# Row sums of two softmaxes on VectorE in place of ScalarE's accumulator, in a two-layer decoder

## What is computed

```python
def _layernorm(x, axis=-1, eps=1e-05):
    m = jnp.mean(x, axis=axis, keepdims=True)
    v = jnp.var(x, axis=axis, keepdims=True)
    return (x - m) / jnp.sqrt(v + eps)
...
    def _L0_xattn_ref(query, key, value, cell_mask, seq_mask, W_k, b_k, W_o, b_o):
        ...
        k_proj = jnp.einsum('bkd,qd->bkq', key, W_k) + b_k
        scores = jnp.einsum('bqd,bkd->bqk', query, k_proj)
        scores = scores + jnp.log(cell_mask) + jnp.log(seq_mask)[:, None, :]
        p_attn = jax.nn.softmax(scores, axis=-1)
        x = jnp.einsum('bqk,bkd->bqd', p_attn, value)
        return jnp.einsum('bqd,od->bqo', x, W_o) + b_o
...
    def _L1_xattn_ref(query, key, value, Wq, bq, Wk, bk, Wv, bv, Wo, bo):
        ...
        Q = jnp.einsum('bsd,de->bse', query, Wq) + bq
        K = jnp.einsum('bsd,de->bse', key, Wk) + bk
        V = jnp.einsum('bsd,de->bse', value, Wv) + bv
        scale = 1.0 / jnp.sqrt(jnp.asarray(D, Q.dtype))
        scores = jnp.einsum('bqd,bkd->bqk', Q, K) * scale
        attn = jax.nn.softmax(scores, axis=-1)
        out = jnp.einsum('bqk,bkd->bqd', attn, V)
        return jnp.einsum('bsd,de->bse', out, Wo) + bo
...
    x = _layernorm(x + _L0_attn_ref(x, L0_attn_w_qkv, L0_attn_w_conv1), axis=-1)
    x = _layernorm(x + _L0_xattn_ref(x, ctx_1024, ctx_1024, mask_BxSxS2_ff1, mask_BxS2_ff1, L0_xattn_W_k, L0_xattn_b_k, L0_xattn_W_o, L0_xattn_b_o), axis=-1)
    x = _layernorm(x + _L0_ffn_ref(x, L0_ffn_Wg, L0_ffn_Wq, L0_ffn_Wk, L0_ffn_Wv, L0_ffn_Wo), axis=-1)
    x = _layernorm(x + _L1_attn_ref(x, L1_attn_Wq, L1_attn_bq, L1_attn_Wk, L1_attn_bk, L1_attn_Wv, L1_attn_bv, L1_attn_Wo, L1_attn_bo), axis=-1)
    x = _layernorm(x + _L1_xattn_ref(x, ctx_1024, ctx_1024, L1_xattn_Wq, L1_xattn_bq, L1_xattn_Wk, L1_xattn_bk, L1_xattn_Wv, L1_xattn_bv, L1_xattn_Wo, L1_xattn_bo), axis=-1)
    x = _layernorm(x + _L1_ffn_ref(x, L1_ffn_w_int8, L1_ffn_weight_scale, L1_ffn_bias), axis=-1)
```

## Time and profile before

| | us |
|---|---|
| median of 3 runs | 848.61 |
| lowest and highest | 847.72, 851.18 |
| the profiled execution's own time | 853.0 |
| its span in the trace | 851.1 |

### The profile page before, as it was taken

How to read it: one execution, slowest core, us unless ns; L and a number is a source line. 1 busy time by engine, 2 the same in 40 slices (tenths; PEclk the granted TensorE clock), 3 DMA queues, 4 the chain that set the end, 5 groups by cost and what they waited for, 6 DMA issues and landing times.

```text
span 851.1 us, 20772 instructions
## 1 busy us (share of the span) xinstructions
PE 785.4 (92%) x8013; PEld 606.1 (71%) x8013; DVE 654.7 (77%) x1973; ACT 488.7 (57%) x1509; POOL 359.3 (42%) x604
## 2 busy tenths in 40 slices
PE   8989999998887999999989899999999899999992
PEld 4566787765766778766767688776777688777771
DVE  6163888787787698788778779789769879888676
ACT  3126445686556445577655554588655645587654
POOL 0088312306676523403775632402777633202465
PEclk7799999999999999999999999999999999999996
DMA  9893000001353000000236000001244200000001
GB/s 222 240 288 154 2 2 2 1 3 56 113 191 135 23 2 2 1 3 29 97 134 220 29 12 2 1 2 29 60 170 154 78 2 2 2 2 2 2 1 39
DMA packets 23074, 53.31 MB, mean 63 GB/s; under 512 B 3888, under 2 KB 9680, under 8 KB 22976
## 3 DMA queue, kind: packets, MB, share of 16 engines
q1 hardware_dynamic: 22976, 51.99, 19.1%
HBM read 48.67 MB, written 3.31 MB: 61 GB/s over the span
## 4 chain that ended last, share of the span: by engine, by line
PE 64%; DVE 16%; POOL 8%; ACT 7%; issue 3%; DMA 1%; SPq 0%; DVEq 0%; ACTq 0%; POOLq 0%
PE psum L429 11%; PE psum L434 11%; PE psum L473 8%; PE psum L630 5%; PE psum L652 5%; PE psum L459 4%; PE psum L643 4%; DVE bn L930 2%; ACT x L710 2%; POOL rstd L1199 2%; PE psum L466 2%; PE psum L565 2%; POOL xplus L1206 1%; PE psum L424 1%; PE psum L574 1%
## 5 line engine op out<-in xcount | busy, mean ns | idle before, releaser
L710 ACT ACTIVATE x<-res,ez,rstd 100x256 f32<-100x256 f32 x160 | 86.7, 593 | 65.4 <-POOL ez L1202 65.2
L473 PE MATMUL psum<-eT,ctx 128*128 128x100 f32 x768 | 95.2, 280 | 1.3 <-DVE eT L956 1.3
L473 PEld LDWEIGHTS psum<-eT,ctx 128*128 128x128 f32 x768 | 92.4, 197 | 2.5 <-DVE eT L956 1.7
L1197 POOL TENSOR_SCALAR ve<-mv 100x2 f32<-100x2 f32 x96 | 22.4, 233 | 163.2 <-DVE mv L933 159.1
L704 ACT ACTIVATE eT<-psum 100x400 f32<-100x400 f32 (+3 forms) x128 | 61.7, 495 | 43.7 <-PE psum L466 19.5
L459 PE MATMUL psum<-ctxT,qT 128*100 128x361 f32 x256 | 84.9, 474 | 1.5 <-ACT qT L704 1.1
L816 ACT ACTIVATE work<-psum,mx 100x100 f32<-100x100 f32 x256 | 67.5, 365 | 21.7 <-DVE mx L1112 21.5
L1185 POOL TENSOR_TENSOR kT<-cell,kT 100x722 f32<-100x722 f32 x12 | 20.7, 1722 | 131.5 <-ACT cell L684 131.5
L704 ACT ACTIVATE xT<-psum 128x400 f32<-128x400 f32 (+2 forms) x80 | 35.5, 445 | 69.0 <-PE psum L589 25.7
L1199 POOL TENSOR_TENSOR rstd<-ve,minus_half 100x2 f32<-100x2 f32 x96 | 70.1, 730 | 8.0
L930 DVE BATCH_NORM_STATS2 bn<-res 100x6 f32<-100x256 f32 x192 | 71.2, 412 | 0.0
(11 more groups left out here) (243 smaller groups left out, 2028.1 us busy)
## 6 DMA issues: line engine op xcount, KB each, us to landing
ctx<-in_ctx SPq DMA_DIRECT2D x16, 768.0 KB, 7.0
ctxT<-in_ctxT SPq DMA_DIRECT2D x16, 722.0 KB, 5.0
cell<-in_cell SPq DMA_DIRECT2D x12, 282.0 KB
seq<-in_seq SPq DMA_DIRECT2D x12, 282.0 KB
x<-in_x SPq DMA_DIRECT2D x16, 200.0 KB
out<-vs SPq DMA_DIRECT2D x16, 200.0 KB
eT<-agent_rows SPq DMA_DIRECT2D x12, 200.0 KB
work<-in_x SPq DMA_DIRECT2D x4, 384.0 KB
```

What stands on the lines that cost most here:

```text
L473: last = e.matmul(bk[b][:, c * S:(c + 1) * S], s.ctx[:, b, j, c * P:(c + 1) * P], s.pT[:, b, j, :], start=j == 0, stop=j == S2C - 1)
L710: e.activation(dst[0:S, b, :], s.res[0:S, b, :], ACT.Identity, scale=s.rstd[:, b:b + 1], bias=s.shift[:, b:b + 1]).then_inc(*act.up(f"x{b}"))
```

## The change

Three edits and a table. ScalarE's exponential loses `accum_out`. VectorE gets a `tensor_reduce` with add, over 100 x 2 x 361 elements of `s.p`, that writes both batches' sums at once; it stands behind the wait for the second exponential, raises a new step "su", and the reciprocal waits for this step. The step lists of the stages first and second on VectorE get the name "su". The sequences of all five engines are new.

```diff
--- before.py
+++ after.py
@@ -85,10 +85,10 @@
     "start": "bias weights",
     "mask": "zero clip",
     "mix": NORM,
-    "first": "mx0 nb0 mx1 nb1 pT0 rs aT1 " + NORM,
+    "first": "mx0 nb0 mx1 nb1 pT0 su rs aT1 " + NORM,
     "pick": "z0 z1 gp gt tie0 tie1 rk0 rk1 pk0 pk1 kT vs1 mx0 su0 mx1 su1 sm0 sm1 rd eT1 aT " + NORM,
     "local": "k0 k1 k2 k3 v1 " + " ".join(f"ma{i} mb{i} eT{i} rd{i} aT{i}" for i in range(NB * NC)) + " " + NORM,
-    "second": "mx0 nb0 mx1 nb1 pT0 rs aT1 " + NORM,
+    "second": "mx0 nb0 mx1 nb1 pT0 su rs aT1 " + NORM,
     "quant": "am am2 am3 sc y0 y1 up0 up1 yq0 yq1 os " + NORM,
 }
 GPSIMD = {
@@ -738,8 +738,7 @@
                 for b in range(NB):
                     e.wait_ge(*dve(f"nb{b}", t))
                     src = s.p[:, b, 0:S2] if stage == "first" else bk[b][0:S, 0:S2]
-                    e.activation(s.p[:, b, 0:S2], src, ACT.Exp, bias=s.nbias[:, b:b + 1],
-                                 accum_out=s.sum[:, b:b + 1]).then_inc(*act.up(f"ex{b}"))
+                    e.activation(s.p[:, b, 0:S2], src, ACT.Exp, bias=s.nbias[:, b:b + 1]).then_inc(*act.up(f"ex{b}"))
                     yield
                 e.wait_ge(*pe("pT1", t))
                 copy(s.pT[:, 1, :, :].rearrange("p j t -> p (j t)"), bk[1][:, 0:S2C * S]).then_inc(*act.up("pT1"))
@@ -956,6 +955,8 @@
                 e.tensor_copy(s.pT[:, 0, :, :].rearrange("p j t -> p (j t)"), bk[0][:, 0:S2C * S]).then_inc(*dve.up("pT0"))
                 yield
                 e.wait_ge(*act("ex1", t))
+                e.tensor_reduce(s.sum[:, :], s.p[:, :, 0:S2], AX, ALU.add).then_inc(*dve.up("su"))
+                e.wait_ge(*dve("su", t))
                 e.reciprocal(s.rsum[:, :], s.sum[:, :]).then_inc(*dve.up("rs"))
                 e.wait_ge(*pe("av1", t))
                 e.tensor_copy(s.aT[:, :, S:2 * S], bk[1][:, 0:NC * S].rearrange("p (c t) -> p c t", c=NC)).then_inc(
@@ -1409,39 +1410,39 @@

...
-        "BACDABABCBCADADBCBAABDCAACABCDCBCBDADDACDDABABCAABBACADCBBACDABBCACDBDCBCABCDDADCBDAADACBDBDAACBACAC"
...
+        "BACDABBABCCADADCBDAABACBAACBDBCCCBDADDCDADABABCAABBACADCBBACBDACACBDBDCBACBCDDACADDBADACBDAADBCBACCD"
...
```

More of the change, by code:

```diff
@@ L1411 @@
     "PE": (
-        "BACDABABCBCADADBCBAABDCAACABCDCBCBDADDACDDABABCAABBACADCBBACDABBCACDBDCBCABCDDADCBDAADACBDBDAACBACAC"
-        "DCBDBCABDDBCACBACBDCBABCCBCDADCDACDBABCADBCDABACADCBCADBCABDDABDCDADBADAAAADABCBBDBCBBABABCCDCDCCDCC"
-        "BAABADDDADADBDBACCAABBABBCCDBDBCABACACACCDCCDAABDBBDCBABBADDDCDDACBCADBACDCDBDCBCABDDCACADBADCADBDBA"
-        "BCDACCBADCACBBDBDCADBCDCABCABDADBCDBAACDABCADBDCABDCABCADCABBCBDDAACBADCADCAABCBAABABCDDCDBBBDBCBDAA"
-        "DCCDCCBBCDACADDDAADDBAACACBAABBBBBBCDCDBACAACACCCCDCDBADBABDBACDDDDADCBBACACBDCCADBDCBDBACBDDCADCABD"
@@ new lines @@
+        "ACBDCBABDDBCACBCADBCBABDCCBCDACDACDABCBABDCDABACADCBCACDBABDABDDCDABADDAAADAABCBBDCBBBAABBCCDCDCCDCA"
+        "BCABDADDADDDABBACCAABBABBBDCCDBCABCAAACCCDCACDABDBBBDABBCDDCDDADACACBBDCACDDBDCBACBDDCACABDADCADBBDA"
+        "BCDACBACCDACBBDBACDDBCDCBACABDADBCDBAACDABCADBDCABDACBCADCACDBBBDAABCADACDCBAABCAABACBDDCDBBBDBCBDAA"
+        "DCDCCCBBDACACDDADDBADAACCBAAABBBBBCBCDDACBAACCACCCDCDABDBABBDACDDDCDADBBACACDBCCADBDCBDBCABDDCACABDD"
+        "ACDBBCDADBCCAABACBDACBDBDBACCADCADBBCBADDBDACADCACBABDDCBDAABCACDBACDBDCABDACBACCDBACBAAADAADBCBBDCD"
@@ new lines @@
+        "BABBBACDCDCCCCDABCBAAADDDDADADBCACAABBBBBBDCDCBACABCAACDCCCCDAABDBABDDBCADDDDBABCACBCBDACBDCDBDCACBD"
+        "DCABCADADCADBDAABCDABCABDCCBCBDACBCDADBCDABCDBADBDCABCADACBBADCDABDABACCDCABCBDDBDCABCADCACADABADBAA"
+        "ACDBCBDCBBBBACCDBDACCDCCDDDDBDDBCCDD"),
+    "DVE": (
+        "BACBDCDCADAAABBBCCDACAADBDACBCABADBCDBDCBACACAAADADBBDAACBABBCBABBCCBDDCCCCBDCDDADDDAADACBADBACCBABA"
+        "DCBCBCADBBCDACBACDBACBCDBCCDADABDCAABCDABBCACDACACDDBBBDBDDDAAACDACADABABBADBDBBCCACACBBCDCBDDCAABDA"
+        "DCDCAABDBCBDABDBAACABCCDACACBCBABCADDABBACDCBADBABDDACBDDCDABBCCCBCDCDCBDDCDAADDDACADBABDCBACBACCABD"
+        "BDBCCBADDABCCADBADBBACDDACAABDCCBDABBCAADCADCCBBBDBAADCACDDCCABABABDDDBDBAABACCBCADBCBDCDCBAADCDACDC"
+        "AAABDBBCDBABADACCBCDAACBCBCBDDCACAADBACDDABADBABDBDCCBDCABBCBCDCDCCBDCDADDDDCDABAADBCABABCCBACABDCBA"
+        "DBCADBDCBCADABDBADCADCABDACCBDABBAADDCACBDCCBDBBACACDADCCAAADBBDBAADBDBBCACCBACBCDBCDABDCAADCDDACAAD"
+        "CBBBDADABACDBCCABCACBCBABDDCACBDBACDADAADABBDBBDCCBBDABCCDCCDCCBDCDADDDADCAADBADBACBBACACBCDBCADBBCD"
+        "DACCBADABDBCABDADCABACDCBADBACDBDCACBDCBDCBDCDAAACADAABDBABDCACBBCBACBDDCCDBDCDDBDCDCD"),
@@ new lines @@
+    "ACT": (
+        "BAABCBADAACBADBCDBACBDDCACACBBCDCDADABDBACACBABADADCCBAABBCADBDBCADCBCADACDBACBDDAABDACCBCDDCBDABABC"
+        "CDACBBDBCCACDBDACBACBCDDADAABCCBABCADADAADBBDADAACDABCBBAABCBCBBACDDCCBDCABCDADABDACADBDACDABABACBDB"
+        "DBCBBCDBCACACCADACCDACBDBDCDCBDBADBADDBCAACBDCDADDBCBCACBDACDADBCDABBDACDBACACDBCDBBADCAADCCBBDDDBCA"
+        "CACABBBDDDAAACCCBBADDBACDAABACCAABABCADBBCBDCBDBACABDDCDABBCCDADCCADBAADBDADCCABAABCDADBBCBBBCBCAADC"
+        "CACCADCBCDDBADDCBDDCBAADBADCABDCBDACDCBDBCADBACCABDDDCBDBCADBCCAAADBCDBCDBACAADCBBBDDCDAAACCBBDDBADA"
+        "CACBCBADBDDAACCAACBABBADDABBCADCBACBABBCDCADDCBCBCACDADABAADBDACDCADAABCBDDBCBBBBACDCABCDCCAACDCDACB"
+        "BDDACBDBDCADBADACDBBDCBACBDDACBCDACCBADBDCDADABACDABCCDDBCBBACCADACDBBDDBCDACAACBBDDBADAACCCBBDBDDCA"
+        "CACADABAADBDAABCBCBAACBCBCDBCADDCBDACBDDDDCCBDDBCDCD"),
@@ L1439 @@
     "POOL": (
-        "BABCAADCDBABCCDDABCDABACBADCDBDACAAABBBABCCCABDAACDCDBADBBADACBCCBDBDCDCACDBDDCADABACBDCADDCBAAABABB"
-        "BCCCBCADAADCDBABDBDABACBCCDBDCDACCDBDDCADBACBDABCACDDAAABABBBCBCCACDAADCDBDABBADABCCCBBDCDDACCDDDBCA"
-        "DBACBADCDDBACAABCBBACAACDDBBDABCCCDBDDCD"),
+        "BABCAADCDBABCDCDABCDABAACBDACBDCDAAABBBABCCCABDAACCDDBABBDADACBCCBDBDCDCACDBDDCADABACBDBCACDAADABBAB"
+        "BCCCBCDAAADDBCADBBDABACBCCDBCDDACCDBDDCADBAACBADCCDAABABABBBCBDCCACDAADCDBDABBADABCCCBBDCDDACCDDDBCA"
@@ L1443 @@
+        "DBACBABDCDACABACBCBADAACDDBABDBCCCDBDDCD"),
     "SP": (
-        "ABCDAABCABACDBCDDBCDAABBCADACBCDDBCDABABCACBDDDCBACD"),
+        "ABCDABABAACCDCDBDBCDABABACBCDCADDBCDABACBACDDCBDABCD"),
 }
```

20 lines of the change are left out of this document (removed).

## The result

The changed kernel takes 862.86 us, median of 3 runs (859.42 to 863.64), against 848.61 before: a ratio of 1.0157, 95% interval 1.0111 to 1.0203. That is 14.3 us slower. The prediction was 850.5 us with a range to 858.5: wrong in size, and outside its range.

What follows compares the result with a forecast made beforehand. TensorE, busy 785.4 of 851.1 us, was taken as the bound, so only work in front of it counts. Reads -2.4 and remaining sums +4.3 make +1.9 us: 848.6 becomes 850.5 us, 8-in-10 range 843 to 858.5.

Steps and rivals of the forecast that it cites:

- The order at 0 +-3 us: New interleaving of the four streams in the engines' sequences: no block of TensorE's work saved, priced 0 +-3 us.
- The reads, -2.4 us: 64 accumulator reads leave ScalarE; TensorE released 0.10 us earlier in 24 waits for exponentials: 2.4 us gained, bounds 0 to 4.6.
- 12 us less busy time: Sign that the forecast is right: ScalarE's busy time down by 12 us.
- the 21.3 us that I had named: Sign that the forecast is right: TensorE's wait for the exponentials near 21 us, from 23.9 before.
- The sum, 0.90 us: Each of VectorE's 32 new sums over 722 columns takes 0.90 us, priced from the maximum; cheap alternative near 0.6.
- Hidden, 10.0 us: On VectorE the sums fill 10.0 us of the 17.5 us that the copy aT waited in 14 places.
- The rest, 20.4 x 0.21 = 4.3 us: The 20.4 us of sums left in VectorE's queue, priced by its chain share over busy share, 0.21: 4.3 us lost.
- The sums land on TensorE: Slower rival, chance 0.32: sums not in VectorE's waits delay other streams and reach TensorE; ten of 18 give +7.1, about 855.7 us.
- The exponential was the bottleneck: Faster rival, chance 0.20: earlier release and new order take 8.0 us off TensorE's wait for exponentials, sums cost 2: 842.6 us.

Runs made afterwards that it cites:

- nosum_oldorder: The kernel before without the accumulator and without any row sum (the reciprocal reads a tile of ones), old sequences: 852.58 us, ratio 1.0016.
- sum_oldorder: The changed kernel with all five sequences of the kernel before (sums on VectorE, no accumulator reads): 857.25 us, ratio 1.0055 against the kernel before.

## Why the prediction was wrong, point by point

- **The order at 0 +-3 us** is the step that failed. It measured +14 us. I had compared the two tables at three places, found no block of TensorE's work that moved as a whole, and took that for small. But three of the five stretches pay 3.4 to 4.5 us each, some 40% of it as idle time of TensorE, none of it longer than 2.3 us at once. "Nothing stands out" was no bound: 980 of the 2666 letters differ, which lost 1.7% here, and my +-3 rested on no row.
- **The reads, -2.4 us.** The overlap was read rightly: ScalarE's busy time fell by 5.9 us, near the 6.4 of the queue and far from the 12.3 by the column, for 64 reads. My term for what would show it, 12 us less busy time, contradicted my own reading. The step from the queue to the path was too large: 24 waits x 0.10 took each wait as shortened by the whole 0.10, but with the reads alone gone the wait fell from 23.9 to 23.3 us. The timed gain can't be told from 0 (nosum_oldorder +0.16% +-0.44) and is about 1 us with the clock's share taken off. That the changed kernel's wait came to the 21.3 us that I had named is no confirmation: with the old table and no reads it is 23.0 and 23.3, with the new table and the reads 23.4.
- **The sum, 0.90 us.** Measured 0.894. The Trainium skill says in "VectorE: DVE Perf Modes", section "The perf-mode tier table", that a tensor_reduce has no faster form; the trace agrees, at 1.2 ns a column against 0.80 of the comparison.
- **Hidden, 10.0 us.** With the table kept the waits in front of aT fell by 11.7, near the forecast. The 10.6 between the two kernels agree by luck: the new table first made the waits 22.5, and the sums filled 15.6 of them.
- **The rest, 20.4 x 0.21 = 4.3 us.** In the old sequences the sum and the missing reads together cost +4.7 +-3.8, and the sum alone some 5.5 (sum_oldorder against nosum_oldorder: 5.2 by the means, 5.7 +-1.4 with the clock's share taken off): about right in size. The rate was not: it held for the first sum only, and a share of the chain over a share of busy time says nothing of the next 28 us, which cost 0.7 to 0.9 each.
- **The rivals.** "The sums land on TensorE" gave 855.7 us and the right sign by another mechanism: in the changed kernel TensorE waits 0.9 us for what stands behind the sums. Its figure is nearly that of the old sequences with the sum (+0.55%, 853.3). "The exponential was the bottleneck" fell: the wait got 2.6 us shorter and the kernel no faster. I had put an order built on the change into the rival that gains. With the new table the sums cost nothing that can be timed, but the table itself costs 14 us.
- **The range** would have held the sum alone and left no room for the table, the larger part of the diff.

What stays open: why the new table has more idle time everywhere. It is shown that it does, in which stretches, that it isn't SyncE's string, and that none of the three moves that were tried brings it back. The strings of the other four engines were not exchanged one at a time. That the waits in front of aT are what takes the sums fits the sums' filling 15.6 us of them; that these waits are bought with the idle times elsewhere is argued, not shown. No version beats the kernel before, and even a sum for nothing would gain no more than the reads' 1 us (nosum_oldorder, 1.0016).
